# Cross attention on one core: gamma and beta applied per partition after the transpose, and the fp16 halves of z and k made by GpSimd

## What is computed

```python
mu = mean(x, -1); var = var(x, -1)
z = (x - mu) * rsqrt(var + 1e-5) * ln_gamma + ln_beta
Q = split_heads(z @ Wq.T);  K = V = split_heads(ctx)
scores = einsum('bhsd,bhtd->bhst', Q, K) * HEAD_DIM ** -0.5     # + mask
attn = einsum('bhst,bhtd->bhsd', softmax(scores), V)
out = x + attn @ Wout.T
```

## Time and profile before

| | us |
|---|---|
| median of three runs | 628.84 (628.08 to 629.17) |
| the profiled execution, its own time | 630.9 |
| its span (first to last instruction) | 629.1 |
| PE / DVE / ACT / POOL busy | 583.6 / 380.1 / 457.0 / 80.7 |

### The profile page before, as it was taken

One profiled execution on the slowest core, in us unless ns is written; L12 is line 12 of the kernel. 1 busy time (PEld: TensorE's weight loads), 2 busy tenths in 40 slices (PEclk: granted clock), 3 DMA queues, 4 the chain that ended last, 5 costly groups with the idle time before them and its releaser, 6 DMA issues.

```text
span 629.1 us, 12713 instructions
## 1 busy us (share of the span) xinstructions
PE 583.6 (93%) x4768; PEld 394.2 (63%) x4768; DVE 380.1 (60%) x813; ACT 457.0 (73%) x1377; POOL 80.7 (13%) x38
## 2 busy tenths in 40 slices
PE   3698597999999999999999999999999999998897
PEld 3587365665776558765776567665776567644443
DVE  6857677468663795368654785378654782278211
ACT  2633889789856986689767986689767985699740
POOL 2405000410023000600032000600041000000000
PEclk9899789999999999999999999999999999999899
DMA  8769212452424332443334252343244232321202
GB/s 339 263 214 196 68 34 87 109 146 85 120 73 121 113 104 102 118 118 98 107 111 123 72 162 57 107 118 108 96 117 128 66 100 56 98 52 67 71 2 101
DMA packets 37023, 69.65 MB, mean 111 GB/s; under 512 B 8833, under 2 KB 10081, under 8 KB 36962
## 3 DMA queue, kind: packets, MB, share of 16 engines
q1 hardware_dynamic: 36962, 68.84, 36.9%
HBM read 34.61 MB, written 8.39 MB: 68 GB/s over the span
## 4 chain that ended last, share of the span: by engine, by line
PE 66%; DVE 12%; ACT 11%; SPq 4%; issue 3%; DMA 3%; DVEq 0%
PE mm L369 20%; PE mm L394 17%; PE pv L448 10%; PE score L436 9%; ACT score L560 9%; PE score L412 6%; DVE nmax L706 5%; SPq L152 2%; PE pv L334 2%; DMA x_nat<-in_x 2%; DVE o_buf L748 1%; PE pv L349 1%; ACT probs L577 1%; SPq L171 1%; PE score L305 1%
## 5 line engine op out<-in xcount | busy, mean ns | idle before, releaser
L560 ACT ACTIVATE score<-score,nmax 128x256 f32<-128x256 f32 x512 | 231.7, 475 | 16.3 <-DVE nmax L706 15.5
L706 DVE TENSOR_REDUCE nmax<-score 128x2 f32<-128x512 f32 x256 | 163.9, 684 | 46.2 <-PE score L412 45.7
L369 PE MATMUL mm<-zT,wqT 128*128 128x256 f16 x1536 | 185.1, 274 | 2.0 <-DVE zT L657 2.0
L394 PE MATMUL mm<-woT,aT 128*128 128x512 f16 x768 | 183.6, 379 | 1.5 <-DVE o_buf L748 1.5
L577 ACT ACTIVATE probs<-score 128x1024 f32<-128x1024 f32 x128 | 123.9, 1022 | 73.3 <-PE score L436 73.0
L369 PEld LDWEIGHTS mm<-zT,wqT 128*128 128x128 f16 x1536 | 150.1, 98 | 23.6 <-issue 2.9
L394 PEld LDWEIGHTS mm<-woT,aT 128*128 128x128 f16 x768 | 74.7, 98 | 73.1 <-DVE o_buf L748 4.4
L560 ACT ACTIVATION_READ_ACCUMULATOR score<-score,nmax 128x1 f32 x512 | 120.5, 235 | 0.0
L741 DVE TENSOR_TENSOR aT<-pv,aT 128x256 f16<-128x256 f32 x64 | 26.9, 423 | 114.6 <-ACT aT L583 113.8
L412 PE MATMUL score<-k_stack,q_stack 97*128 97x256 f16 x512 | 78.8, 277 | 17.0 <-ACT score L560 13.9
L287 POOL TENSOR_TENSOR x_nat<-x_nat,gamma_b 128x1024 f32<-128x1024 f32 x16 | 42.7, 2666 | 391.8 <-DVE x_nat L697 391.8
(11 more groups left out here) (46 smaller groups left out, 327.2 us busy)
## 6 DMA issues: line engine op xcount, KB each, us to landing
k_stack<-kT SPq DMA_DIRECT2D x192, 64.0 KB, 2.0
q_stack<-qT SPq DMA_DIRECT2D x192, 64.0 KB, 2.1
x_nat<-in_x SPq DMA_DIRECT2D x8, 1024.0 KB, 5.5
ctx_sb<-in_ctx SPq DMA_DIRECT2D x8, 1024.0 KB, 6.5
res<-in_x SPq DMA_DIRECT2D x32, 256.0 KB, 3.1
out<-o_buf SPq DMA_DIRECT2D x32, 256.0 KB, 2.1
probs<-in_L_xattn_Wq SPq DMA_DIRECT2D x8, 512.0 KB, 7.0
probs<-in_L_xattn_Wout SPq DMA_DIRECT2D x8, 512.0 KB, 5.8
```

The lines of the kernel that those rows point to most:

```text
L369: last = pe.matmul(mm[i % 2][:, m2 * S:(m2 + 1) * S], wqT[:, wp, k, m * P:(m + 1) * P], zT[:, zp, k, :], start=(v2 == 0), stop=(v2 == KT * ...
L394: last = pe.matmul(mm[i % 2][:], aT[:, ap, k, st * P:(st + 1) * P], woT[:, wp, k, nh * 512:(nh + 1) * 512], start=(v == 0), stop=(v == O_M ...
L560: last = act.activation(score[n % 2][:, j, :], score[n % 2][:, j, :], ACT.Exp, bias=nmax[:, st, h, j, gl:gl + 1], accum_out=sums[:, st, h, ...
L706: dve.tensor_reduce(nmax[:, st, h, at, gl], score[n % 2][:, at, :], AX.X, ALU.max, negate=True).then_inc(max_done, 1)
```

## The change

TensorE now transposes the normalised x without gamma and beta. After the transpose the hidden index lies on the partitions, so gamma and beta are one number per partition: DVE applies them as z leaves PSUM, in two instructions of 128 x 256 with both numbers read per partition, into a new fp32 tile `t_f32` of two buffers. For k one instruction of 128 x 512 multiplies by `K_SCALE` into the same tile. POOL, which cannot read PSUM, then makes the high part (a copy to fp16) and the low part (a subtraction) from `t_f32`. ACT has no part in z and k any more. gamma and beta are loaded as 16 rows of 128 numbers, transposed by TensorE once and copied by DVE to `gb`. A fill's index `f` counts z and k fills together; TensorE may transpose fill f when `t_f32` of fill f - 2 is written, and DVE may write `t_f32` for fill f when POOL has finished fill f - 2. What waited for `z_lo` or `k_lo` to read zT or kT (the q matmuls, SP's copies of k) now waits for POOL's `split_done`.

```diff
-        gamma_b = sb("gamma_b", [P, D], F32)
-        beta_b = sb("beta_b", [P, D], F32)
+        t_f32 = sb("t_f32", [P, 2, 2, S], F32)
+        gb = sb("gb", [P, 2, KT], F32)
...
+        def z_fill(a, i):
+            return 2 + i if a == 0 else 2 * FILLS * a + i
+        def k_fill(a, i):
+            if a == 0:
+                return i if i < 2 else FILLS + i
+            return 2 * FILLS * a + FILLS + i
...
             def fill_k_stack(a, pa, h):
-                sp.wait_ge(k_lo, a * FILLS + 2 * h + 2)
+                sp.wait_ge(split_done, k_fill(a, 2 * h + 1) + 1)
...
-                    sp.wait_ge(zt_ready, (b + 2) * FILLS)
+                    sp.wait_ge(fill_ready, z_fill(b + 1, 3) + 1)
                     load_x(b + 2)
...
-            sp.dma_start(gamma_b[:], gamma.rearrange("(a d) -> a d", a=1).to_broadcast([P, D])).then_inc(gb_in, DMA)
-            sp.dma_start(beta_b[:], beta.rearrange("(a d) -> a d", a=1).to_broadcast([P, D])).then_inc(gb_in, DMA)
+            sp.dma_start(t_f32[0:KT, 0, 0, 0:P], gamma.rearrange("(k p) -> k p", p=P)).then_inc(gb_in, DMA)
+            sp.dma_start(t_f32[KT:2 * KT, 0, 0, 0:P], beta.rearrange("(k p) -> k p", p=P)).then_inc(gb_in, DMA)
...
-            sp.wait_ge(k_lo, FILLS)
+            sp.wait_ge(split_done, k_fill(0, 3) + 1)
...
-            def scale_and_shift(a):
-                for st in range(ST):
-                    pool.wait_ge(norm_done, a * ST + st + 1)
-                    pool.tensor_tensor(x_nat[:, st], x_nat[:, st], gamma_b[:], ALU.mult).then_inc(gamma_done, 1)
-                    pool.wait_ge(gamma_done, a * ST + st + 1)
-                    pool.tensor_tensor(x_nat[:, st], x_nat[:, st], beta_b[:], ALU.add).then_inc(z_done, 1)
+            def z_split(a, i):
+                f = z_fill(a, i)
+                pool.wait_ge(f32_done, f + 1)
+                if i == 0 and a:
+                    pool.wait_ge(q_ready, a * FILLS)
+                at = slice(2 * i, 2 * i + 2)
+                pool.tensor_copy(zT[:, 0, at], t_f32[:, f % 2]).then_inc(split_hi, 1)
+                pool.wait_ge(split_hi, f + 1)
+                pool.tensor_tensor(zT[:, 1, at], t_f32[:, f % 2], zT[:, 0, at], ALU.subtract).then_inc(split_done, 1)
+            def k_split(a, i):      # the same for kT, behind k_in
...
             def wo_transposes(f):
...
-                    pe.wait_ge(k_lo, 3 + f)
+                    pe.wait_ge(f32_done, k_fill(0, 2 + f) + 1)
...
             def z_transposes(a, i, b):
+                f = z_fill(a, i)
                 if i == 0:
-                    pe.wait_ge(z_done, (a + 1) * ST)
-                if i >= 2:
-                    pe.wait_ge(z_lo, a * FILLS + i - 1)
-                elif b is None:
-                    pe.wait_ge(k_lo, i + 1)
+                    pe.wait_ge(norm_done, (a + 1) * ST)
+                if b is None or i >= 2:
+                    pe.wait_ge(f32_done, f - 1)
...
             def q_matmuls(a, lo, hi, c):
...
                     if u == 0:
-                        pe.wait_ge(z_lo, (a + 1) * FILLS)
+                        pe.wait_ge(split_done, z_fill(a, 3) + 1)
+                    if u == 0 and known(a, 0):
+                        pe.wait_ge(gb_done, 1)
...
             pe.wait_ge(ident_ok, 1)
+            pe.wait_ge(gb_in, 2 * DMA)
+            pe.transpose(mm[0][:, 0:2 * KT], gb_rows, ident[0:2 * KT, 0:2 * KT]).then_inc(gb_ready, 1)
...
-            def z_split(a, i):      # ACT; its k_split goes in the same way
-                act.wait_ge(zt_ready, a * FILLS + i + 1)
-                if i == 0 and not known(a, 0):
-                    act.wait_ge(q_ready, a * FILLS)
-                act.activation(zT[:, 0, 2 * i:2 * i + 2, :], pv[i % 2][:], ACT.Copy).then_inc(z_hi, 1)
...
-            def z_split(a, i):      # DVE; k_split likewise, with K_SCALE
-                dve.wait_ge(z_hi, a * FILLS + i + 1)
-                dve.tensor_tensor(zT[:, 1, 2 * i:2 * i + 2, :], pv[i % 2][:], zT[:, 0, 2 * i:2 * i + 2, :], ALU.subtract).then_inc(z_lo, 1)
+            def z_scale(a, i):
+                f = z_fill(a, i)
+                dve.wait_ge(fill_ready, f + 1)
+                if f >= 2:
+                    dve.wait_ge(split_done, f - 1)
+                for m in range(2):
+                    k = 2 * i + m
+                    last = dve.tensor_scalar(t_f32[:, f % 2, m, :], pv[f % 2][:, m, :], gb[:, 0, k:k + 1], gb[:, 1, k:k + 1], ALU.mult, ALU.add)
+                last.then_inc(f32_done, 1)
+            def k_scale(a, i):      # the same waits
+                dve.tensor_scalar(t_f32[:, f % 2], pv[f % 2][:], K_SCALE, None, ALU.mult).then_inc(f32_done, 1)
...
                 normalise(0, st)
+            dve.wait_ge(gb_ready, 1)
+            dve.tensor_copy(gb[:].rearrange("p a k -> p (a k)"), mm[0][:, 0:2 * KT]).then_inc(gb_done, 1)
+            dve.wait_ge(gb_done, 1)
```

More of the change, by code:

```diff
@@ L86, in xattn @@
         mask_add = k_stack[P - 1:P, 0, 0].rearrange("o j g s -> o (j g) s")[:, 0:B, :]
+        gb_rows = t_f32[0:2 * KT, 0, 0, 0:P]
         w_nat = probs[:].rearrange("p a t j s -> p (a t) (j s)")
@@ L282, in _ @@
                                pattern=[[-1, P]], channel_multiplier=1).then_inc(ident_ok, 1)
-            def scale_and_shift(a):
-                for st in range(ST):
-                    pool.wait_ge(norm_done, a * ST + st + 1)
-                    pool.tensor_tensor(x_nat[:, st], x_nat[:, st], gamma_b[:], ALU.mult).then_inc(gamma_done, 1)
-                    pool.wait_ge(gamma_done, a * ST + st + 1)
-                    pool.tensor_tensor(x_nat[:, st], x_nat[:, st], beta_b[:], ALU.add).then_inc(z_done, 1)
-            pool.wait_ge(gb_in, 2 * DMA)
-            scale_and_shift(0)
+            def z_split(a, i):
[8 more added lines that the diff above has]
+            def k_split(a, i):
+                f = k_fill(a, i)
+                pool.wait_ge(f32_done, f + 1)
+                if i % 2 == 0 and a:
+                    pool.wait_ge(k_in[i // 2], a * (STACK + 1) * DMA)
+                at = slice(2 * i, 2 * i + 2)
+                pool.tensor_copy(kT[:, 0, at], t_f32[:, f % 2]).then_inc(split_hi, 1)
+                pool.wait_ge(split_hi, f + 1)
+                pool.tensor_tensor(kT[:, 1, at], t_f32[:, f % 2], kT[:, 0, at], ALU.subtract).then_inc(split_done, 1)
+            for i in (0, 1):
+                k_split(0, i)
+            for i in range(FILLS):
+                z_split(0, i)
+            for i in (2, 3):
+                k_split(0, i)
             for a in range(1, B):
-                scale_and_shift(a)
+                for i in range(FILLS):
+                    z_split(a, i)
+                for i in range(FILLS):
+                    k_split(a, i)
         @block.tensor
@@ L501, in _ @@
             for i in (0, 1):
-                k_transposes(0, 0, i, None)
+                k_transposes(0, 0, i)
             for i in range(FILLS):
@@ L534, in wo_split @@
                                ACT.Copy, scale=W_SCALE).then_inc(wo_hi, 1)
-            def k_split(a, i):
-                act.wait_ge(kt_ready, a * FILLS + i + 1)
-                if i % 2 == 0 and not known(a, 0):
-                    act.wait_ge(k_in[i // 2], a * (STACK + 1) * DMA)
-                act.activation(kT[:, 0, 2 * i:2 * i + 2, :], pv[i % 2][:], ACT.Copy, scale=K_SCALE).then_inc(k_hi, 1)
-            def z_split(a, i):
-                act.wait_ge(zt_ready, a * FILLS + i + 1)
-                if i == 0 and not known(a, 0):
-                    act.wait_ge(q_ready, a * FILLS)
-                act.activation(zT[:, 0, 2 * i:2 * i + 2, :], pv[i % 2][:], ACT.Copy).then_inc(z_hi, 1)
             def q_split(a, i):
@@ L586, in iteration @@
                 for n in range(STEPS):
-                    if not last:
-                        if n in Z_STEPS:
-                            z_split(b + 1, Z_STEPS.index(n))
-                        if n in K_STEPS:
-                            k_split(b + 1, K_STEPS.index(n))
                     if first and n == Q_STEP_FIRST:
@@ L615, in _ @@
                 wq_split(f)
-            for i in (0, 1):
-                k_split(0, i)
-            for i in range(FILLS):
-                z_split(0, i)
-            for i in (2, 3):
-                k_split(0, i)
             for m in range(KT):
@@ L809, in _ @@
             for i in (0, 1):
-                k_split(0, i)
+                k_scale(0, i)
             for i in range(FILLS):
-                z_split(0, i)
+                z_scale(0, i)
             for i in (2, 3):
-                k_split(0, i)
+                k_scale(0, i)
             for m in range(KT):
```

46 lines of the change are left out of this document (20 added, 26 removed).

## The result

| | before | after |
|---|---|---|
| median, six runs each, us | 629.14 (628.08 to 632.3) | 634.2 (633.01 to 635.37) |
| ratio | | 1.0066 (95%: 1.004 to 1.0092) |
| span of the profiled execution | 629.1 | 633.6 |

The account below looks back on a forecast made before the run. The prediction took PE to bound batches 1 to 6. Its terms, +1.3 + 0.9 - 1.8 + 0.5 + 3.9 = +4.8 us, took the median from 628.84 to 633.6, range 626.8 to 640.5.

Parts of the forecast that it names:

- What bounds the kernel: Batches 1 to 6: PE bounds them, idling 1.03 us in each; sparing ACT there can win no more than 6.2 us.
- Part 2: DVE's scaling: k 0.68 us, z's two instructions 0.68 to 0.85 overlapped; zero cost, DVE not in the chain in steps 1 to 4.
- Part 3: POOL's time for one fill: copy 0.75, subtraction 1.2, in all 2.05 us (1.8 to 2.6); zero cost in batches 1 to 6.
- 2.5 us lower: The sum if POOL's copy ran at the skill's one-input rate, 0.43 us, making a fill 1.75 us.
- Part 4: Before batch 0: faster mask instruction, -2.3, against waiting for six POOL fills and lost PE clock, 1.9; start +1.3 us.
- Part 5: Batch 0: q matmuls of step 4 start later, +0.9 us (0 to 3); ACT spared its copies, -1.8 (-2.3 to 0).
- Part 6: `lse_half` in step 10: DVE's L718 waits for POOL's copy, 0.65 us a batch, +3.9 in batches 1 to 6, 0.5 in batch 0.
- no conflict: Rival: in `lse_half` DVE does not wait for POOL; +0.4, 629.2 us (627.6 to 631); chance 0.27.
- Faster: Rival: POOL's copy takes 0.5, PE's clock before batch 0 is not lost, no conflict; -2.8, 626.0 us; chance 0.14.
- slow copy: Rival: POOL needs 2.6 us a fill, delaying start and batch 0 and lengthening `lse_half`'s conflict; 642.5 us; chance 0.11.
- both L718: Rival: in `lse_half` the second L718 also waits, for POOL's subtraction; 1.2 more in each of seven batches, 642 us; chance 0.11.
- fills that hold PE: Case: POOL makes z and k too late in batches 1 to 6, needing more than 3.5 us a fill; chance 0.01.

Follow-up runs that it names:

- e10: The changed kernel with z scaled by one DVE instruction with a constant, gamma and beta left out; pitch 70.17 us against 70.28, one run.
- e2: The kernel before with one wait added: POOL's second operation of batch 0 also waits for DVE's mask instruction; ratio to the kernel before 0.9952.
- e4: The changed kernel with 56 unused transposes of the identity on PE while it waits for POOL before batch 0; ratio to the kernel before 1.0051.
- e3: The changed kernel with the q matmuls in batch 0's score stage begun at step 6 instead of 4; ratio to the kernel before 1.0013.
- e5: The changed kernel with k split by ACT and DVE straight from PSUM as before, z still through POOL; ratio to the kernel before 1.0015.
- e1: The changed kernel with `lse_half` put before the scaling of k3 on DVE in step 10; ratio to the kernel before 1.0038.
- e8: The kernel before with one unused POOL copy of 512 fp32 SBUF columns added per batch, just before `lse_half`; pitch 70.17 us against 69.90, one run.

## Why the prediction was right or wrong

**What bounds the kernel: right.** Batches 1 to 6 gained nothing from what ACT was spared: it was busy 51.30 us of a batch instead of 54.92, and the pitch rose by 0.38. (3.6 less, not the 4.8 of the forecast, which added durations that overlap their neighbours'.) No run with ACT relieved has a pitch under 69.90.

**Part 2, DVE: mostly right.** k's scaling has 0.68, as taken. z's two take 0.99 from start to end, above the upper bound of 0.85. The bound came from L741 (423 ns), which has two inputs and one arithmetic operation; L662 has one input, two operations and two numbers per partition, and takes 535 - 423 = 112 ns more. Which of these costs it no run separates. The cover that was named, DVE not in the chain in steps 1 to 4, was not whole: z2's transposes start 0.07 late and cost 0.116 a batch (e10), 0.7 in all, where I had zero: 0.7 us too little.

**Part 3, POOL: right in kind, high by 0.26.** Copy 0.61 (0.75 taken), subtraction 1.16 (1.2), a fill 1.79 (2.05, and a lower bound of 1.8). The estimate from the one-input rate of the Trainium skill (GPSIMD Engine Reference, § Engine selection), 0.43 for the copy and 1.75 for the fill, is low for the copy (0.61) and near for the fill. The "2.5 us lower" that I gave with it does not follow from my own terms: 6 x 0.30 at the start, up to 0.9 in batch 0 and 7 x 0.32 in the conflict make nearly 5. It was not part of the sum.

**Part 4, the start: right in kind, with errors that cancel.** L824, the mask, takes 1.21 (1.1), k0 is scaled at 25.2 (25.4), z is complete at 36.1 (37.8), the lost clock costs 2.3 (1.9), batch 0 starts at 67.43 (67.7). Against the 1.6 that POOL's faster fills give stand 0.4 more of lost clock, 0.6 of waits for DVE at the Wout transposes that I had counted gone, and 0.3 ahead of the first scores. e2 and e4 show gain and loss apart. Since the start of one and the same code varies by 1.1, that +1.0 came near the forecast's +1.3 proves little.

**Part 5, batch 0: wrong, +2.5 instead of -0.4** (with part 6's share). The failed step is the start of the q matmuls, +0.9. I counted four fills of POOL from the first z on, as if POOL led and its fills began as early after the batch's start as before. POOL was faster than that, and DVE led: the last z half leaves DVE no earlier than before (78.95, 11.5 after the start; before, 77.5, 11.1 after), and POOL adds its whole 1.9 behind it. The rule would have been the later of two times, four fills from the first or one fill from the last; the second gives +2.3, which is what the matmuls at 80.91 show (80.91 - 77.60 - 1.01). e3 takes this out by moving them (3.4 in all, with 1.2 of the conflict). The other terms: the copies of ACT are worth 1.3 (e5 against e1, and what is left of 2.3 + 1.5 - 2.5), where I had 1.8, and the conflict in `lse_half` costs 1.5 (part 6), where I had 0.5. So +0.9 - 1.8 + 0.5 was +2.3 - 1.3 + 1.5.

**Part 6, the conflict: right in mechanism and place, half in size.** In batches 1 to 6 0.26 instead of 0.65, 1.6 us in all instead of 3.9. Two things made it less. The copy takes 0.61 instead of 0.75, and I let the first L718 wait too, but it goes through (0.16) and only the second waits for the rest of the copy. In batch 0, 0.5 had been taken and it is 1.5 (2.07 against 0.58; e1 takes back 0.8 and leaves 0.66): there L728 waits for the copy and the second L731 for the subtraction, and the upper bound of 1.9 was the nearer.

So the sum met the measurement by luck: against the forecast part 6 in batches 1 to 6 gave -2.3, batch 0 +2.9, z's scaling +0.7, the start -0.3, and the clock in batch 7, which has nothing to do with the change, -1.3. Together that is -0.3. The rivals: no conflict is refuted by e8. Faster did not occur, though POOL's fills were as fast as it asked (1.79): the clock was lost and the conflict was there. The slow copy did not occur, nor both L718, except that batch 0 looks like the latter. (The chances of the five cases add to 1.00 without the 0.01 given to fills that hold PE, a slip without effect.)

## What to carry to other kernels

An engine's share of busy time does not tell what its work is worth: 30 us taken off ACT won nothing in the six batches where PE led, and what took over the work sat behind the producer with its full latency. For a consumer that waits for the last of several pieces, take the later of "all pieces at the new engine's rate" and "last piece as now, plus one piece of the new engine". Before moving work to GpSimd, look at what VectorE does at that moment: its operations with two inputs in SBUF (L731), and here also a one-input one from SBUF to SBUF (the mask), were held up by GpSimd's operations that read SBUF, and a change of order or one added wait took most of the cost away. And before reading a difference of a microsecond in one profiled execution, look at what kernels with the same code up to that point have there: here the start varied by 1.1 us and the clock's return in batch 0 by 1.0.

## What the runs showed of the hardware that I had not expected

- A DVE operation that starts after POOL's recorded start is not always the one that waits. With POOL's copy from 301.23, the first L731 at 301.40 took 0.16 and the next, 0.1 behind it, 0.47. In batch 0, with POOL's subtraction from 96.06, the first L731 at 96.06 took 0.17 and the next, 0.09 behind it, 1.13; but L728 at 95.39, 0.02 after the copy's recorded start at 95.37, took 0.64 instead of 0.18. So operations at offsets of 0.17 and 0.00 passed and those at 0.02 and 0.09 did not. No single delay from POOL's recorded start fits these rows; what decides stays open.
- A DVE `tensor_scalar` with two per-partition numbers and two operations takes 535 ns for 256 columns of PSUM, 0.11 us more than a two-input operation of that size (L741).
- Work whose result nobody uses kept PE's clock up. From 25 us to the first q matmuls PE was busy 50% in the changed kernel (5.62 of 11.18 us, mean clock 0.61), and the 24 q matmuls ran at 0.51; with the 56 transposes it was busy 90% (9.94 of 11.00 us, clock 1.00), and they ran at full clock.
- A one-partition instruction of 2048 elements took 3.41 us for its own 1.21, with nothing in the waits view that names POOL as what DVE waited for: only its duration and POOL's timeline beside it show it.
